# Turning the feed-forward's input with VectorE blocks and memory transfers instead of TensorE transposes

## The chip, the cores and the metric

One Trainium2 (trn2) chip; the kernel runs on 1 of its cores. The metric is the device time of one execution in microseconds, as the median of the runs. The engines are named as in the profile: PE (TensorE; PEld its weight loads), DVE (VectorE), ACT (ScalarE), POOL (GpSimd) and SP (SyncE, which issues all DMAs here; SPq is its queue).

## What is computed

x has 4096 tokens (2 sequences of 2048) of 256 features. An attention block with hierarchical decay (16 heads, 12 levels), a residual and a layer norm come first; a gated two-step cell over the two sequences, a residual and a layer norm follow. Everything is fp32.

```python
x = L0_attn_x                                    # (2, 2048, 256)
x = layernorm(x + attention(x, ...))             # 16 heads, chunks of 128 tokens in the kernel
# feed-forward: a scan over the first axis (2 steps), then one output product
ft = sigmoid(xt @ wf.T + c @ uf.T + bf)
it = sigmoid(xt @ wi.T + c @ ui.T + bi)
gt = tanh(xt @ wc.T + c @ uc.T + bc)
c  = ft * c + it * gt
h  = tanh(x @ wo.T + c_final @ uo.T + bo)
out = layernorm(x + h)
```

## The kernel before

**Tiles.** The normalised result of the attention stands in SBUF as `xs`, 32 chunks (`ci`) of 128 tokens, tokens on the partitions, 256 features along the row. The feed-forward needs x with features on the partitions, so it must be turned. It works in 4 blocks (`blk`) of 512 tokens for each of the two sequences (`t`); block (blk, t) holds the four chunks from 16t + 4 blk on. Every product is made of three (`mm3`): each operand is split into a rounded high part (`wH`, `yH`, by ACT) and the rest (`wL`, `yL`, by DVE or POOL).

**Turning before.** `turn_block(blk, t)` exists on three engines. PE makes 8 transposes (2 halves `k` of the features, 4 chunks) through `tr` (L386) into two PSUM banks; ACT copies each bank to `yH` (fp32r); DVE subtracts `yH` from the bank to give `yL`. Then `gate_x` multiplies them with the weights.

**Order.** Each engine's program is written out by hand over steps `s` from -3 to 140; a chunk of attention takes four steps. An engine works strictly in the order of its program and stands at a wait until the semaphore is there. Chunk ci is normalised by DVE in `outer_norm(ci)` at step 4ci + 11, so chunk 28 at step 123, chunk 29 at 127, and 31 at 135. The feed-forward begins at step 127 (`FIRST_FFN`) and is laid out as groups by `ffn_groups()`, one group a step: first the turns of (0,0) and (0,1), then gate products; the turns of the later blocks stand in later groups.

**ACT near the seam.** At steps 119 to 126 ACT splits the eight feed-forward weights, `split_ffn(0)` to `split_ffn(7)`, and at step 124 (ahead of `split_ffn(5)`) it makes the exponentials `E` of the last chunk (31), for which PE's scores of that chunk wait. So the splits of weights 2, 3 and 4 stand ahead of these exponentials in ACT's program. PE's `first_bias` (36 products of two columns) follows at step 126 and needs weights 3 to 5. POOL subtracts for `wL` behind ACT.

**SP's queue.** For each pair of chunks `sg` it stores and reloads the coefficients (`load_coefs`: one store to `scr`, then 8 broadcast loads of 64 KB for each chunk), then issues `load_xt(sg + 3)` and `load_x(sg + 2)`. Weights 0 and 1 are loaded at sg 13 and 14; after sg 15 come `load_wf(2)` to `load_wf(7)`, each after the `wL` two before it, since `xt` has two buffers; then the output stores.

Of the kernel before, what the change touches and what calls it, by code (L numbers as in the profile page):

```python
# [5 lines left out]
P = 128  # L6
F32 = mybir.dt.float32
F32R = mybir.dt.float32r
# [136 lines left out]
TURN = {u[1:]: n for n, u in enumerate([u for u in UNITS if u[0] == "t"])}  # L145
YUSE = {u: n for n, u in enumerate([u for u in UNITS if u[0] == "t" or (u[0] == "o" and u[1] < 16)])}

# [8 lines left out]
def program(nc, x, xT, wqk, wtok, wout, wffn, cst, bcv, fv, out):  # L156
    ctx = ExitStack()
    with ctx:
        scr = nc.dram_tensor("scr", (8, 8, 2, 128), F32, kind="Internal").ap()

        def sb(name, shape, dt=F32):
# [17 lines left out]
        oo = sb("oo", [P, 256])  # L179
        x1 = sb("x1", [P, 256])  # L180
        st1 = sb("st1", [P, 6])
        mv1 = sb("mv1", [P, 2])
# [50 lines left out]

        yH, yL = [[[sb(f"{n}{t}{i}", [P, 2, 512], F32R) for i in range(2)] for t in range(2)] for n in ("yH", "yL")]
        gb = [[sb(f"g{i}{n}", [P, 512]) for n in range(3)] for i in range(2)]
# [8 lines left out]
        ring = [banks[0:3], [banks[3], banks[6], banks[7]]]  # L244

        def turned(blk, k):

            return banks[4 + k] if blk or not k else banks[6]


# [14 lines left out]
        l_xt = [sem(f"l_xt{i}") for i in range(2)]  # L265
        l_sc, l_cB = sem("l_sc"), [sem("l_cB0"), sem("l_cB1")]
        l_x = [sem(f"l_x{i}") for i in range(NSG)]

# [3 lines left out]
        g_v0, g_s0 = sem("g_v0"), sem("g_s0")  # L272
        p_b0, p_turn, p_gate, p_o = sem("p_b0"), sem("p_turn"), sem("p_gate"), sem("p_o")

# [13 lines left out]
        d_b0, d_y, d_c1, d_c2 = sem("d_b0"), [sem("d_y0"), sem("d_y1")], sem("d_c1"), sem("d_c2")  # L288
        d_c2l, d_mv3, d_out = sem("d_c2l"), sem("d_mv3"), sem("d_out")

        g_xl, g_sp, g_vw = sem("g_xl"), sem("g_sp"), sem("g_vw")
# [13 lines left out]
        def _(e):  # L305
# [10 lines left out]
            def load_coefs(sg):  # L316
# [5 lines left out]
                for c in range(2):  # L322
                    ci = 2 * sg + c
                    if ci in INTER:
# [4 lines left out]
                        for a in range(8):  # L329
                            e.dma_start(cB[c][16 * a:16 * a + 16, :, :, :].rearrange("p l u t -> p (l u) t"),  # L330
                                        scr[a, :, c, :].partition_broadcast(16)).then_inc(l_cB[c], 16)

            load_xt(0)
            e.dma_start(wt0, kt(wtok)).then_inc(l_wt, 16)
# [17 lines left out]
            for sg in range(NSG):  # L352
                load_coefs(sg)
                if sg + 3 < NSG:
                    e.wait_ge(g_xl, sg + 1)
                    load_xt(sg + 3)
                if sg + 2 < NSG:
                    load_x(sg + 2)
                if sg >= NSG - 3 and sg < NSG - 1:
                    e.wait_ge(g_xl, sg + 1)  # L360
                    load_wf(sg - NSG + 3)
            for n in range(2, 8):
                e.wait_ge(g_wf, n - 1)
                load_wf(n)
            for n in range(16):
                e.wait_ge(a_out, n + 1)
                if n == 15:
                    e.wait_ge(d_out, 1)
                e.dma_start(ov[:, :, n, :], xs[:, n:n + 17:16, :]).then_inc(l_out, 16)
# [11 lines left out]
        def _(e):  # L381
# [221 lines left out]

            def turn_block(blk, t):
                e.wait_ge(d_x2, 16 * t + 4 * blk + 4)
                if blk == 0 and t == 0:

                    e.wait_ge(d_w, 4 * NC)
                for k in range(2):
                    use = YUSE["t", blk, t]  # L610
                    if use:
                        e.wait_ge(d_y[k], use)
                    elif k == 1:
                        e.wait_ge(m_free[0], len([m for m, u in MISC.values() if m == 0]))
                    if blk == 1 and t == 0 and k == 1:

                        e.wait_ge(d_oo, NC)
                    for q in range(4):
                        y = tr(turned(blk, k)[:, 128 * q:128 * q + 128], xs[:, 16 * t + 4 * blk + q, 128 * k:128 * k + 128])
                    y.then_inc(p_turn, 1)  # L620

            def gate_x(blk, t, mt, n):
                y, idx = blk % 2, 4 * blk + 2 * t + mt
                if idx >= 2:
                    e.wait_ge(a_g, 3 * (idx - 2) + n + 1)
                elif n == 0:
                    e.wait_ge(d_b0, 1)
                if n == 0:
                    e.wait_ge(d_y[1], YUSE["t", blk, t] + 1)
                if idx == 1 and n == 1:  # L630

                    e.wait_ge(d_y[1], 2)
                if idx == 1 and n == 2:
                    e.wait_ge(m_free[1], len([m for m, u in MISC.values() if m == 1]))
                for k in range(2):
                    c = wcol(WF + n, mt)
                    m = mm3(ring[mt][n][:, :], wH[:, k, c], wL[:, k, c], yH[t][y][:, k, :], yL[t][y][:, k, :],
                            k == 0, k == 1 and not t)
                if not t:
                    m.then_inc(p_gate, 1)  # L640
# [25 lines left out]
            def outputs(n):  # L666
                blk, q = n // 4, n % 4
                y, use = blk % 2, YUSE["o", n]
                c = slice(128 * q, 128 * q + 128)
                Ba, Bb = [banks[i] for i in LAST.get(n, (4, 5))]  # L670
                if n in (12, 14, 15):

                    e.wait_ge(a_g, 48 if n == 12 else 51)
                else:
                    e.wait_ge(d_y[1], use if n < 12 else use - 1)
                for t in range(2):
                    for k in range(2):
                        m = mm3(Bb[:, 256 * t:256 * t + 256], yH[t][y][:, k, c], yL[t][y][:, k, c],
                                wH[:, k, wcol(WO)], wL[:, k, wcol(WO)], k == 0, k == 1)
                m.then_inc(p_o, 1)  # L680
                if blk < 3:
                    e.wait_ge(g_c2l, 2 * blk + 2)
                else:
                    e.wait_ge(d_c2l, 2 if n < 14 else 3)
                for k in range(2):
                    m = mm3(Ba[:, 0:256], c2H[y][:, k, c], c2L[y][:, k, c], wH[:, k, wcol(UO)], wL[:, k, wcol(UO)],
                            k == 0, k == 1)
                m.then_inc(p_o, 1)
# [14 lines left out]
            for s in STEPS:  # L703
# [31 lines left out]
                for u in units_at(s):  # L735
                    if u[0] == "x":
                        gate_x(*u[1:])
                    elif u[0] == "c":
                        gate_c(*u[1:])
                    elif u[0] == "h":  # L740
                        gate_h(*u[1:])
                    elif u[0] == "t":
                        turn_block(*u[1:])
                    elif u[1] < 16:
                        outputs(u[1])
# [3 lines left out]
        def _(e):  # L749
# [104 lines left out]
            def turn_block(blk, t):  # L854
                i = blk % 2
                for k in range(2):
                    e.wait_ge(p_turn, 2 * TURN[blk, t] + k + 1)
                    if blk >= 2 and k == 0:
                        e.wait_ge(p_o, 2 * (4 * (blk - 2) + 4))
                    act(yH[t][i][:, k, :], turned(blk, k)[:, :], ACT.Copy).then_inc(a_yh, 1)  # L860

# [41 lines left out]
            def outputs(n):  # L903
                i = n % 2
                e.wait_ge(d_y[1], YUSE["o", n] + 1)
                act(hh[i][:, :], hh[i][:, :], ACT.Tanh).then_inc(a_hh, 1)
# [73 lines left out]
        def _(e):  # L980
# [159 lines left out]
            def outer_norm(ci):  # L1140
                e.wait_ge(g_rs2, ci + 1)
                e.tensor_scalar(xs[:, ci, :], x1[:, :], mv2[:, 0:1], rs2[:, 0:1], ALU.subtract, ALU.mult).then_inc(d_x2, 1)

            def tokens(sg, j):
                nonlocal made
# [73 lines left out]
            def turn_block(blk, t):  # L1219
                i = blk % 2  # L1220
                for k in range(2):
                    e.wait_ge(a_yh, 2 * TURN[blk, t] + k + 1)
                    tt(yL[t][i][:, k, :], turned(blk, k)[:, :], yH[t][i][:, k, :], ALU.subtract).then_inc(d_y[k], 1)

# [35 lines left out]
            def outputs(n):  # L1260
                i, use = n % 2, YUSE["o", n]
                Ba, Bb = [banks[i] for i in LAST.get(n, (4, 5))]
                e.wait_ge(p_o, 2 * n + 2)
                if n >= 2:
                    e.wait_ge(d_y[1], YUSE["o", n - 2] + 1)
                tt(cu[i][:, :], Ba[:, 0:256], bv[:, B_BO:B_BO + 256], ALU.add).then_inc(d_y[0], 1)
                h3 = hh[i][:, :].rearrange("p (t n) -> p t n", t=2)
                e.wait_ge(d_y[0], use + 1)
                if n >= 2 and n - 2 != 13:
# [40 lines left out]
            for s in STEPS:  # L1310
# [37 lines left out]
                if (ci := chunk_at(s, 11)) is not None:  # L1348
                    outer_norm(ci)


# [224 lines left out]
```

## Time and profile before

| | |
|---|---|
| median of the runs | 687.79 us (687.26 to 689.74, 3 runs) |
| profiled execution | 687.91 us, span 686.1 us |
| mean granted clock of PE | 0.985 |
| PE busy | 665.7 us (97%) |
| DVE / ACT / POOL busy | 474.0 / 339.3 / 348.1 us |
| DMA | 53588 packets, 37.09 MB |

All times of the rows below are from the start of the span. In a timeline row stand start, duration, engine, line of the kernel, operation, result and operands, how many instructions are merged, and in brackets how long the engine was idle before and on whom it waited last. A clock of 1.00 is the 2.4 GHz level of PE, 0.50 the 1.2 GHz level.

### The profile page before, as it was taken

How to read it: one execution, taken by the hardware profiler on the slowest of the kernel's cores; microseconds unless marked ns; L12 is line 12 of the kernel's file. 1: busy time of each engine (PE TensorE's matmuls, PEld its weight loads, DVE VectorE, ACT ScalarE, POOL GpSimd, SP SyncE). 2: the span in 40 equal slices, each digit the busy share in tenths (PEclk: the TensorE clock that was granted, in tenths of full speed). 3: DMA queues.
4: the chain of work that ended last, by engine and by line, in shares of the span. 5: the costliest groups of instructions: out<-in, count | busy, mean ns of one | idle time of the engine just before them, and what ended most of it. 6: DMA issues, size and time to landing. Idle time of an engine off the chain costs nothing.

```text
span 686.1 us, 22147 instructions
## 1 busy us (share of the span) xinstructions
PE 665.7 (97%) x9194; PEld 602.8 (88%) x9194; DVE 474.0 (69%) x1072; ACT 339.3 (49%) x759; POOL 348.1 (51%) x471
## 2 busy tenths in 40 slices
PE   9999999999999999999999999999978999999994
PEld 7889999999999999899999999999967788888894
DVE  3765786869786868658696868688896445454546
ACT  5565444454555454544545555545433434555555
POOL 2715563647556565556474555665455215343434
PEclk9999999999999999999999999999997899999998
DMA  9213030302222130203031221303032000000002
GB/s 299 61 29 91 8 97 8 94 24 76 50 51 55 46 83 18 67 6 95 22 79 47 54 52 48 88 13 84 2 99 62 1 1 1 32 32 32 32 32 92
DMA packets 53588, 37.09 MB, mean 54 GB/s; under 512 B 5360, under 2 KB 52080, under 8 KB 53488
## 3 DMA queue, kind: packets, MB, share of 16 engines
q1 hardware_dynamic: 53488, 35.67, 19.1%
q8 instruction: 73, 1.20, 0.8%
q14 instruction: 27, 0.22, 0.1%
HBM read 30.41 MB, written 5.24 MB: 52 GB/s over the span
## 4 chain that ended last, share of the span: by engine, by line
PE 90%; DVE 3%; ACT 2%; SPq 1%; DMA 1%; issue 1%; POOL 1%; DVEq 0%; ACTq 0%; POOLq 0%
PE bank L383 66%; PE bank L386 6%; PE bank L407 5%; PE bank L474 5%; PE bank L439 5%; PE bank L503 4%; SPq L330 1%; DMA xt<-in_wffn 1%; DVE t L985 1%; ACT t L751 1%; ACT E L751 0%; DVE t L988 0%; DVE st L1285 0%; DVE hh L985 0%; DMA scr<-cT 0%
## 5 line engine op out<-in xcount | busy, mean ns | idle before, releaser
L383 PE MATMUL bank<-xH,wH 128*128 128x256 f32 x480 | 144.4, 301 | 1.2 <-ACT KT L751 0.9
L383 PE MATMUL bank<-xL,wH 128*128 128x256 f32 x480 | 135.0, 281 | 0.0
L383 PE MATMUL bank<-xH,wL 128*128 128x256 f32 x480 | 134.4, 280 | 0.0
L985 DVE TENSOR_TENSOR W<-bank,E 128x512 f32<-128x512 f32 x128 | 82.2, 685 | 31.3 <-PE bank L383 31.3
L383 PEld LDWEIGHTS bank<-xH,wH 128*128 128x128 f32 x480 | 90.4, 188 | 7.6 <-issue 7.0
L383 PEld LDWEIGHTS bank<-xL,wH 128*128 128x128 f32 x480 | 90.6, 189 | 0.4
L383 PEld LDWEIGHTS bank<-xH,wL 128*128 128x128 f32 x480 | 90.5, 188 | 0.0
L751 ACT ACTIVATE E<-bank 128x512 f32<-128x512 f32 x128 | 66.1, 604 | 47.7 <-PE bank L407 47.7
L751 ACT ACTIVATE QT<-bank 128x512 f32<-128x512 f32 x64 | 38.2, 596 | 101.3 <-PE bank L383 101.3
L383 PE MATMUL bank<-QT,KT 64*128 64x128 f32 x1024 | 65.8, 278 | 1.6 <-ACT E L751 1.6
L383 PEld LDWEIGHTS bank<-QT,KT 64*128 64x128 f32 x1024 | 59.7, 188 | 6.0 <-ACT E L751 1.8
L751 ACT ACTIVATE KT<-bank 128x512 f32<-128x512 f32 x64 | 38.0, 594 | 51.4 <-PE bank L383 51.4
L1357 POOL TENSOR_TENSOR lr<-mv,cs 128x1 f32<-128x1 f32 (+1 forms) x80 | 18.2, 227 | 80.9 <-DVE mv L1138 75.0
L1357 POOL TENSOR_TENSOR rs<-lr,cs 128x1 f32<-128x1 f32 (+1 forms) x80 | 51.7, 647 | 6.3
L1357 POOL TENSOR_TENSOR x<-oo,xs 128x256 f32<-128x256 f32 x32 | 23.5, 735 | 60.3 <-DVE oo L988 57.7
L1357 POOL TENSOR_TENSOR t<-t 128x416 f32<-128x416 f32 x42 | 46.6, 1110 | 3.4
L985 DVE TENSOR_TENSOR g<-g 128x512 f32<-128x512 f32 (+1 forms) x26 | 17.6, 676 | 38.3 <-ACT g L751 38.0
L407 PE MATMUL bank<-CT,AT 32*128 32x128 f32 x1024 | 38.1, 286 | 5.7 <-DVE CT L1212 4.1
L751 ACT ACTIVATE t<-t 128x416 f32<-128x416 f32 x64 | 35.3, 552 | 14.2 <-DVE t L1170 10.4
L1357 POOL TENSOR_TENSOR prod<-ll,cs 128x512 f32<-128x512 f32 x32 | 40.7, 1272 | 1.2 <-DVE ll L985 1.2
L1357 POOL TENSOR_TENSOR xL<-xt,xH 128x512 fp32r<-128x512 f32 x15 | 19.1, 1273 | 41.4 <-ACT xH L751 41.4
L383 PE MATMUL bank<-yH,wH 128*128 128x512 f32 (+1 forms) x102 | 40.1, 393 | 0.0
(151 smaller groups left out, 1678.0 us busy)
## 6 DMA issues: line engine op xcount, KB each, us to landing
cB<-scr SPq DMA_DIRECT2D x240, 64.0 KB, 2.9
xt<-in_xT SPq DMA_DIRECT2D x16, 256.0 KB, 2.9
xs<-in_x SPq DMA_DIRECT2D x16, 256.0 KB, 3.2
out<-xs SPq DMA_DIRECT2D x16, 256.0 KB, 2.1
xt<-in_wffn SPq DMA_DIRECT2D x8, 256.0 KB, 3.1
QT<-in_wqk SPq DMA_DIRECT2D x4, 256.0 KB, 5.8
KT<-in_wqk SPq DMA_DIRECT2D x4, 256.0 KB, 7.1
scr<-cT SPq DMA_DIRECT2D x16, 64.0 KB, 1.9
```

Source lines behind the costliest of these rows:

```text
L330: e.dma_start(cB[c][16 * a:16 * a + 16, :, :, :].rearrange("p l u t -> p (l u) t"), scr[a, :, c, :].partition_broadcast(16)).then_inc(l_cB ...
L383: return e.matmul(o, a, b, start=start, stop=stop)
L386: return e.transpose(o, i, ident)
L407: m = e.matmul(XP[q][:, :].rearrange("p (h t) -> p h t", h=H)[:, :, 8 * j:8 * j + 8], AT[b][r, j, :], CT[b][r, :].rearrange("p (h t) -> p ...
L439: y = e.matmul(YB[32 * n:32 * n + 32, 128 * k:128 * k + 128], V[sg % 3][:, c, v:v + 32], W[:, h, :], start=u == 0 and k == 0, stop=u == 1, ...
L474: t = e.matmul(MB[MISC["inter", ci, k][0]][32 * n:32 * n + 32, 128 * i:128 * i + 128], S[r, l, n, 16 * o:16 * o + 32], QT[b][r, 4 * o + n, ...
L503: t = e.matmul(MB[m][k:k + 64, 16 * q:16 * q + 16], Kt[:, 128 * q + k:128 * q + k + 64], Vw[b][:, c, 128 * h + 16 * q:128 * h + 16 * q + 1 ...
L751: return e.activation(o, i, f, **kw)
L985: return e.tensor_tensor(o, a, b, op)
L1357: return e.tensor_tensor(o, a, b, op)
```

## The change

The eight transposes of a block leave PE. After `outer_norm(ci)` DVE turns the chunk in blocks of 32x32 (`turn_result`, one `transpose` of 128x256 into one of two buffers `tx`); SP stores that to a scratch tensor `xscr` in memory (128 rows of 1 KB), and `load_turned(blk, t)` brings a block back with features on the partitions: 8 DMAs, each 32 partitions x 16 x 32 numbers, that is 512 runs of 128 bytes. ACT and DVE split `yT` from SBUF in place of the PSUM banks. PE's `turn_block` and its wait on the normalisation go; the wait for the last `W` moves to the first gate product. Semaphores and memory are added accordingly; `yT` has one buffer for each t, so a load waits for the split of the block before (`d_yl`).

In SP's queue `store_turned(2 sg - 3)` and `store_turned(2 sg - 2)` stand behind `load_coefs(sg)`, `load_turned(0, 0)` behind `load_wf(2)` and `load_turned(0, 1)` behind `load_wf(3)`; blocks 1 and 2 come after `load_wf(7)`, block 3 after the first two output stores.

```diff
+            def store_turned(ci):
+                e.wait_ge(d_tx, ci + 1)
+                e.dma_start(xscr[4 * ci:4 * ci + 4, :, :].rearrange("i f c -> (i f) c"), tx[ci % 2][:, :]).then_inc(
+                    l_tx[ci % 2], 16)
+
+            def load_turned(blk, t):
+
+                c0 = 16 * t + 4 * blk
+                for i in range(2):
+                    e.wait_ge(l_tx[i], 16 * (c0 // 2 + 2))
+                if blk == 0:
+
+                    e.wait_ge(p_proj, 8 * NSG)
+                else:
+                    e.wait_ge(d_yl, TURN[blk - 1, t] + 1)
+                s4 = xscr[4 * c0:4 * c0 + 16, :, :].rearrange("g f (k j t) -> j f k g t", k=2, j=4)
+                for j in range(4):
+                    for k in range(2):
+                        e.dma_start(yT[t][32 * j:32 * j + 32, k, :].rearrange("f (g t) -> f g t", g=16),
+                                    s4[j, :, k, :, :]).then_inc(l_yT[t], 16)
...
             for sg in range(NSG):
                 load_coefs(sg)
+                for ci in (2 * sg - 3, 2 * sg - 2):
+                    if ci >= 0:
+                        store_turned(ci)
                 if sg + 3 < NSG:
...
             for n in range(2, 8):
                 e.wait_ge(g_wf, n - 1)
                 load_wf(n)
+                if n in (2, 3):
+                    load_turned(0, n - 2)
+            for blk in (1, 2):
+                for t in range(2):
+                    load_turned(blk, t)
+                for ci in (NC - 3, NC - 2) if blk == 1 else (NC - 1,):
+                    store_turned(ci)
             for n in range(16):
+                if n == 2:
+                    for t in range(2):
+                        load_turned(3, t)
...
             def gate_x(blk, t, mt, n):
                 y, idx = blk % 2, 4 * blk + 2 * t + mt
                 if idx >= 2:
                     e.wait_ge(a_g, 3 * (idx - 2) + n + 1)
                 elif n == 0:
                     e.wait_ge(d_b0, 1)
+
+                    e.wait_ge(d_w, 4 * NC)
                 if n == 0:
-                    e.wait_ge(d_y[1], YUSE["t", blk, t] + 1)
...
+                    e.wait_ge(d_yl, TURN[blk, t] + 1)
...
+            def turn_result(ci):
+
+                e.wait_ge(d_x2, ci + 1)
+                if ci >= 2:
+                    e.wait_ge(l_tx[ci % 2], 16 * (ci // 2))
+                e.transpose(tx[ci % 2][:, :], xs[:, ci, :]).then_inc(d_tx, 1)
```

## Rows read from the trace of the kernel before

**Rows 1.** The page's part 4: shares of the span in the chain, by line

```profile
PE bank L383 66%; PE bank L386 6%; PE bank L407 5%; PE bank L474 5%; PE bank L439 5%; PE bank L503 4%; SPq L330 1%; DMA xt<-in_wffn 1%; DVE t L985 1%; ACT t L751 1%; ACT E L751 0%; DVE t L988 0%; DVE st L1285 0%; DVE hh L985 0%; DMA scr<-cT 0%
```

**Rows 2.** The chain in order of time, 560 on: start, us, what

```profile
560.07 0.87 PE bank L386 x8
...
630.79 0.87 PE bank L386 x8
```

**Rows 3.** Timeline 526 to 536, where attention ends and the feed-forward begins

```profile
528.68 1.97 PE L386 MATMUL bank<-cs,xs 128*128 128x128 f32 x8
528.86 0.16 DVE L985 TENSOR_TENSOR b<-bank,fvs 128x6 f32<-128x6 f32 x1 [0.81 <-PE bank L383]
...
530.46 0.69 DVE L985 TENSOR_TENSOR yL<-bank,yH 128x512 fp32r<-128x512 f32 x1 [1.44 <-ACT yH L751]
...
533.17 1.94 PE L439 MATMUL bank<-W,V 128*32 128x128 f32 x32
...
535.04 0.80 PE L383 MATMUL bank<-yH,wH 128*128 128x512 f32 x1
```

**Rows 4.** Stretches: length, busy us by engine, PE's clock, DMA share, GB/s

```profile
466.00:476.00 10.00, 10.00 (x152) 9.24 (x153) 8.24 (x18) 6.54 (x15) 7.07 (x9) 1.00 0.47 96
584.00:588.00 4.00, 4.00 (x28) 3.64 (x27) 1.76 (x4) 1.52 (x4) 1.55 (x4) 1.00 0.20 66
514.00:516.00 2.00, 2.00 (x34) 1.52 (x34) 1.93 (x4) 0.00 (x0) 1.92 (x3) 0.51 0.40 118
528.00:530.00 2.00, 2.00 (x10) 2.00 (x11) 0.21 (x2) 0.17 (x1) 1.87 (x3) 0.50 0.00 0
```

**Rows 5.** Timeline of SP's queue, 439 to 524: start and length of the issues

```profile
439.65 3.70 SPq L330 DMA_DIRECT2D cB<-scr  x8
...
508.50 14.28 SPq L313 DMA_DIRECT2D xt<-in_wffn  x6
```

**Rows 6.** Timeline of ACT, 511 to 526

```profile
511.78 1.30 ACT L751 ACTIVATE wH<-xt 128x512 fp32r<-128x512 f32 x2 [7.46 <-DMA xt<-in_wffn]
516.86 0.63 ACT L751 ACTIVATE wH<-xt 128x512 fp32r<-128x512 f32 x1 [3.78 <-DMA xt<-in_wffn]
517.39 2.04 ACT L751 ACTIVATE E<-bank 128x512 f32<-128x512 f32 x4
...
525.20 0.63 ACT L751 ACTIVATE wH<-xt 128x512 fp32r<-128x512 f32 x1 [2.94 <-DMA xt<-in_wffn]
```

**Rows 7.** Timeline of DVE, 475 to 516, and of POOL at 512

```profile
475.58 0.59 DVE L988 SCALAR_TENSOR_TENSOR t<-pre,t 128x416 f32<-128x416 f32 x1 [1.05 <-POOL t L1357]
...
491.69 1.29 DVE L985 TENSOR_TENSOR W<-bank,E 128x512 f32<-128x512 f32 x2 [1.73 <-PE bank L383]
...
500.38 0.74 DVE L985 TENSOR_TENSOR S<-S,dec 128x256 f32<-128x256 f32 x2
...
513.01 2.44 DVE L985 TENSOR_TENSOR S<-S,dec 128x256 f32<-128x256 f32 x2
...
515.82 0.41 DVE L1142 TENSOR_SCALAR xs<-x,mv,rs 128x256 f32<-128x256 f32 x1
...
512.49 2.69 POOL L1357 TENSOR_TENSOR wL<-xt,wH 128x512 fp32r<-128x512 f32 x2 [2.14 <-ACT wH L751]
```

**Rows 8.** Timeline of PE, 500 to 519

```profile
500.63 1.08 PE L439 MATMUL bank<-W,V 128*32 128x128 f32 x32
...
512.16 1.78 PE L407 MATMUL bank<-CT,AT 32*128 32x128 f32 x32 [3.82 <-DVE CT L1212]
513.87 1.94 PE L439 MATMUL bank<-W,V 128*32 128x128 f32 x32
...
518.51 2.13 PE L383 MATMUL bank<-QT,KT 64*128 64x128 f32 x32 [1.59 <-ACT E L751]
```

**Rows 9.** Groups by line, engine and form: count, busy us, mean ns, idle before

```profile
L985 DVE TENSOR_TENSOR W<-bank,E 128x512 f32<-128x512 f32 x128 | 82.2, 685 | 31.3 <-PE bank L383 31.3
...
L1212 DVE STREAM_TRANSPOSE CT<-C 128x512 f32<-128x512 f32 x32 | 22.8, 711 | 1.1
```

## What I expect, and why

> **What bounds the kernel now.** I read the chain of work that ended last first, on the page: PE's lines hold 91% of the span, 66% its product line L383 and 6% L386, the line through which every TensorE transpose goes [rows 1]. Work taken from PE is therefore worth its full time wherever PE is the chain. Second, the same chain in order of time over the feed-forward: PE without a break up to 668, with a piece "L386 x8" of 0.87 us six times, the first at 560.07 and the last at 630.79 [rows 2]. Each is one block of 512 tokens being turned. Third, the timeline at the seam between attention and feed-forward, where the first two blocks are turned: PE turns at 528.68, but the first gate product starts only at 535.04 [rows 3]. Fourth, the queues that the change adds work to: SP's DMA issues [rows 5], what ScalarE waits for behind them [rows 6], VectorE and GpSimd [rows 7] and PE [rows 8] from 500 to 525. That last reading decides the case.
>
> **What is removed: six turns inside the feed-forward.** PE is the chain there, so 6 x 0.87 = 5.2 us go [rows 2], if the turned data is there in time. It should be: a pair of loads is issued as soon as the block before has been split, some 28 us before its own use (560.07 against about 532, where the first split ends [rows 2, 3]), and a pair needs about 14 us (below). ScalarE's copy and VectorE's subtraction stay, now from SBUF, where a subtraction can be slowed by GpSimd as below; neither engine is the chain there. Cost 0; if that cover is gone, the price is the same 5.2 us back.
>
> **What is removed at the seam.** Before, from the end of the bias products (528.68) to the first gate product (535.04) pass 6.4 us: two turns, their copies and subtractions, then the last chunk's weighing (1.94) [rows 3]. After the change PE goes from the bias to the weighing at once. Beside that, VectorE adds the bias (0.16) and makes two subtractions (0.69 each), 1.5 us and a few hand-overs; ScalarE's copies can run before, since it idled from 525.8 on [rows 3, 6]. So 1.9 to 2.0 us remain of 6.4: a gain of 4.4 us. Two things take from it. The 32 weighing products took 1.08 us at 500.63 and 1.94 at 513.87, where the granted clock was 0.51 (the 1.2 GHz level) after PE had stood still for 3.8 us before 512.16 [rows 4, 8]. The wait that I find below makes PE stand still longer, so the scores and the inter-chunk products that follow it start at that level: some 3.8 us (512.16 to about 516) at half speed, 1.8 us lost. And the gate products start sooner after the bias stretch, in which the clock was at 0.50 too [rows 4], so more of them run slowly: 0 to 1.7 us, I take 0.8. Net gain 1.8 us.
>
> **What is added on VectorE.** 32 transposes of 128x256. One of 128x512 takes 711 ns; a pass over 256 columns takes 0.41 against 0.69 for 512, so 711 - 280 = 430 ns, with the wait for its own normalisation about 0.46 [rows 7, 9]: 15 us in all. It stands right behind the normalisation. What follows there is a wait in both kinds of chunk: 1.73 us for PE's scores in one, 1.05 us for GpSimd in the other [rows 7]. Both are longer than 0.46, so I take 0; the upper bound is what 0.1 us a chunk would make, 3 us. The stores, 32 of 128 KB, are few and long pieces: 0.
>
> The Trainium skill ("VectorE: DVE Perf Modes", The three transpose paths) gives TensorE 390 ns for a 128x128 bf16 transpose and VectorE 311 ns for 32x32 blocks only. Here PE's eight fp32 transposes cost 0.87 us together in the chain, 109 ns each, so the trace disagrees with the first figure as a price. By the rows the 64 turns are worth 7.0 us of PE, by the page's figure 25, and the forecast would be 680 instead of 698; the measurement decides.
>
> **What is added on SP's queue, and who stands behind it.** SP issues in order and waits in order. Up to now load_wf(2) goes out at 508.50, right after the last coefficient loads [rows 5], and ScalarE, waiting, splits that weight at 511.78, 3.3 us later [rows 6]. In the change three things stand ahead of what follows:
>
> - store_turned(28), before load_wf(2): it waits for VectorE to have normalised chunk 28 and turned it. That normalisation is at 515.82 to 516.23. The pair of S products ahead of it took 2.44 us in place of the 0.74 of a chunk before, beside GpSimd's subtractions of wL (512.49 to 515.18) [rows 7]; those are now later, so 1.7 us fall away: normalised at 514.5, turned at 515.0, stored at 515.4, load_wf(2) at 515.5. That is 7.0 us later than 508.50 (8.7 if the 1.7 stay).
> - load_turned(0,0), between load_wf(2) and load_wf(3), and load_turned(0,1), between load_wf(3) and load_wf(4): 8 DMAs each, 512 pieces of 128 bytes in each DMA, so 4096 pieces, 256 to each of 16 DMA engines.
>
> Nothing in the trace moves 128-byte pieces, so I bound them. Issue: eight coefficient DMAs go out in 3.70 us [rows 5], so a load takes 3.7 us at least. Pieces: from 466 to 476, 16 coefficient DMAs of 128 pieces of 512 bytes kept the engines 0.47 busy: 0.47 x 16 x 10 / 2048 = 37 ns a piece. From 584 to 588, one output of 256 pieces of 1 KB: 0.20 x 16 x 4 / 256 = 50 ns [rows 4]. A line through the two gives 24 ns without any bytes and 27 ns at 128 bytes: 256 x 27 = 7.0 us for one load, more than its issue. The ends are 3.7 us (by issue) and 9.5 us (37 ns, as dear as 512 bytes). I take 7.0, since the line goes through both rows.
>
> The weights go through the same queues behind these pieces: load_wf(2) lands at 518.8, then 7.0 + 0.8 (16 pieces of 50 ns) to load_wf(3), and again 7.8 to load_wf(4): 534.4. ScalarE's program has the splits of weights 2, 3 and 4 ahead of the exponentials of the last chunk: its trace shows 516.86 and right behind it 517.39, after 3.78 us of waiting for that DMA [rows 6]. So the exponentials start at 534.9 in place of 517.39, 17.5 us later. PE's scores of chunk 31 wait for them (518.51, 1.59 us idle already now [rows 8]), and all that is left of attention waits for the scores. PE has nothing else to do: the feed-forward's products stand behind in its order and need the weights anyway.
>
> **Sum.** 686.1 + 17.5 - 1.8 - 5.2 = 696.6 us of span; the profiled execution took 687.91 with 1.8 outside its span, and the median of the runs is 687.79, within 0.1 of it. Forecast: 698.4 us. With loads bound by issue (3.7 us each, wf(4) issued at 523.7) the exponentials start 10.1 us later: 691.0. With 9.5 us a load: 703.4; with the 1.7 us of relief gone and 3 us on VectorE, 708.
>
> **The rivals.**
>
> - Faster. The pieces and the stores are hidden: ScalarE reaches the exponentials of chunk 31 no later than now, because the weights land in time. Then only the gains count, 4.4 less 0.7 for the clock at the gates, and 5.2: 687.9 - 8.9 = 679.0. It decides at load_wf(4) landing by about 517, and for that load_wf(2) would have to go out 7 us before the store ahead of it can. For it speaks that PE, not DMA, has the chain; against it, ScalarE's waits of 7.46 and 3.78 us for these very loads [rows 6]: there is no slack to hide them in.
> - No change. The delay is at its least (small pieces free, every issue a little shorter than above: the exponentials 9 us late) and the seam gives its full 4.4 us: 687.9 + 9 - 4.4 - 5.2 = 687.3.
> - Much slower. A piece of 128 bytes costs more than one of 512, say twice the 27 ns: 54 x 256 = 13.8 us a load, 13.6 more for the two: 712.0. The later loads, 28 us a pair against 28 us of time, would then be just in time. No row shows pieces under 512 bytes in number.
>
> The Trainium skill says of this last case ("DMA: Bandwidth & Descriptors", Specifications) that transfers under 512 bytes are not at line rate, being read-modify-write. No run here shows it yet.
>
> **How the numbers follow.** Forecast (690 to 708): 0.68. Much slower: 0.19. No change: 0.06. Faster: 0.07. A measurement of this kernel tells about 0.5% (3.4 us) from no change. Faster is then 0.07, same 0.06, slower 0.87. The range reaches from just under the issue-bound sum, 689, into the dear pieces, 712.
>
> **What would show it.** In the profile after: load_wf(2) issued near 515.5; ScalarE idle for long before wH, put down to the DMA of in_wffn; the first E of chunk 31 near 535; PE idle before its scores some 17 us, at half the clock behind it; VectorE's transposes near 430 ns; no "L386 x8" in the feed-forward, and 5 us less from the first gate product to the end (151.1 us before [rows 3]). The forecast is wrong if the exponentials start before 527, if a load of 4096 pieces takes under 4 or over 10 us, or if PE waits inside the feed-forward.

## The result, and the profile after

| | before | after |
|---|---|---|
| median, runs taken together | 687.52 us | 694.58 us (694.11 to 695.32) |
| ratio | | 1.0101, 95% interval 1.0085 to 1.0117 |
| span of the profiled execution | 686.1 us | 693.6 us |
| mean granted clock of PE | 0.985 | 0.973 |

The changed kernel is 1.0% slower. 698.4 had been forecast, with 689 to 712 as its range. TensorE does less (659.8 us busy in place of 665.7), and the kernel takes longer.

The seam between attention and feed-forward is where to look. First SP's queue in the changed kernel, from 508 on (start, length and number of the issues); it answers [rows 5]:

```profile
508.26 7.88 SPq L337 DMA_DIRECT2D xscr<-tx  x2
516.19 0.43 SPq L315 DMA_DIRECT2D xt<-in_wffn  x1
516.73 4.23 SPq L353 DMA_DIRECT2D yT<-xscr  x8
521.01 0.49 SPq L315 DMA_DIRECT2D xt<-in_wffn  x1
521.61 4.30 SPq L353 DMA_DIRECT2D yT<-xscr  x8
525.95 9.53 SPq L315 DMA_DIRECT2D xt<-in_wffn  x4
```

The two stores (L337) hold the queue for 7.9 us, nearly all of it the wait for chunk 28: the first store goes out at 508.26, the second, that of chunk 28, at 515.81. Weight 2 goes out at 516.19, not 508.50. Then each reload of a turned block (L353, eight DMAs) puts 4.3 us ahead of the next weight. ScalarE stands behind that, in its timeline (in brackets how long it was idle, and on whom it waited), against [rows 6]:

```profile
519.65 0.63 ACT L769 ACTIVATE wH<-xt 128x512 fp32r<-128x512 f32 x1 [15.00 <-DMA xt<-in_wffn]
524.64 0.63 ACT L769 ACTIVATE wH<-xt 128x512 fp32r<-128x512 f32 x1 [4.36 <-DMA xt<-in_wffn]
529.58 0.63 ACT L769 ACTIVATE wH<-xt 128x512 fp32r<-128x512 f32 x1 [4.31 <-DMA xt<-in_wffn]
530.12 2.04 ACT L769 ACTIVATE E<-bank 128x512 f32<-128x512 f32 x4
```

And PE's timeline behind ScalarE, against [rows 8]:

```profile
516.83 1.10 PE L422 MATMUL bank<-cs,KT 128*128 128x128 f32 x8
531.24 3.78 PE L419 MATMUL bank<-QT,KT 64*128 64x128 f32 x32 [13.31 <-ACT E L769]
534.95 3.19 PE L510 MATMUL bank<-QT,S 64*32 64x128 f32 x128
```

The last exponentials start 12.7 us later than before (517.39), PE stands still for 13.3 us, and the scores behind that take 3.78 us in place of 2.13. The clock is in the stretches of the changed kernel (length, busy us by engine, granted clock, DMA share, GB/s):

```profile
517.00:522.00 5.00, 0.92 (x8) 0.68 (x7) 0.00 (x0) 0.63 (x1) 1.26 (x1) 0.83 0.83 155
522.00:527.00 5.00, 0.00 (x0) 0.00 (x0) 0.00 (x0) 0.63 (x1) 1.57 (x3) 0.50 0.84 153
531.00:537.00 6.00, 5.76 (x112) 5.54 (x120) 1.29 (x2) 3.37 (x8) 2.71 (x4) 0.50 0.25 75
537.40:544.00 6.60, 6.60 (x120) 6.13 (x104) 5.57 (x13) 3.07 (x6) 2.55 (x4) 1.00 0.02 5
546.00:551.00 5.00, 5.00 (x12) 3.94 (x13) 1.77 (x4) 0.69 (x1) 0.21 (x1) 0.50 0.49 78
551.00:556.00 5.00, 5.00 (x22) 4.03 (x22) 2.49 (x5) 2.42 (x4) 0.33 (x1) 1.00 0.81 128
```

Scores and inter-chunk products run at 0.50 (the 1.2 GHz level), the bias products after 537.4 at 1.00 (2.4 GHz), and the gate products start at 0.50 again, until 551. Last, the start of the feed-forward in the timeline of all engines, against [rows 3]:

```profile
542.15 2.50 POOL L1388 TENSOR_TENSOR wL<-xt,wH 128x512 fp32r<-128x512 f32 x2
543.04 1.08 PE L475 MATMUL bank<-W,V 128*32 128x128 f32 x32
543.48 3.52 DVE L1007 TENSOR_TENSOR yL<-yT,yH 128x512 fp32r<-128x512 f32 x4
545.94 0.77 PE L419 MATMUL bank<-yH,wH 128*128 128x512 f32 x1 [1.82 <-DVE yL L1007]
```

From there on the chain is PE without a turn in it, where [rows 2] had one of 0.87 us six times; the chain in order of time shows it as one piece:

```profile
545.94 129.61 PE bank L419 x688
```

To compare all kernels I cut each profiled execution at three points: A, the start of the exponentials of chunk 30; B, that of chunk 31; C, the first gate product. The column on the clock is how long it still stood at half just behind C. A moves by up to 1.5 us from run to run, from well before the seam, so the parts behind it say more than the span. Each row is one execution, up to 1.5 us from the median of its kernel (e1 was taken 1.1 below, e6 1.5 above), so the medians decide what a kernel is worth, and the rows only where its time lies.

| kernel | to A | A to B | B to C | C to end | at half clock after C | span |
|---|---|---|---|---|---|---|
| before | 500.77 | 16.6 | 17.6 | 151.1 | 1.4 | 686.1 |
| after | 501.10 | 29.0 | 15.8 | 147.7 | 5.1 | 693.6 |
| e1_both_moved | 501.33 | 18.7 | 14.4 | 146.9 | 3.4 | 681.3 |
| e2_store_late | 501.14 | 23.0 | 15.6 | 147.6 | 4.9 | 687.4 |
| e3_loads_spread | 500.87 | 25.0 | 14.6 | 147.0 | 3.7 | 687.5 |
| e4_turns_added | 501.71 | 15.5 | 16.4 | 151.3 | 1.8 | 684.9 |
| e5_wait_added | 501.84 | 22.7 | 18.1 | 150.5 | 0 | 693.1 |
| e6_loads_later | 502.25 | 16.8 | 13.1 | 147.2 | 4.1 | 679.3 |
| e7_sixth_first | 502.23 | 15.7 | 13.3 | 146.0 | 1.5 | 677.3 |
| e8_filled | 501.40 | 29.5 | 13.1 | 147.3 | 4.1 | 691.2 |
| e9_long_pieces | 502.11 | 27.0 | 15.8 | 147.6 | 5.0 | 692.5 |
| e10_weights_sooner | 501.69 | 15.8 | 16.2 | 146.0 | 1.5 | 679.7 |

After against before: 0.3 + 12.4 - 1.8 - 3.4 = 7.5 us, the whole difference of the spans.

### The profile page after: what moved, and what is told of

The parts are those of the page before. It is cut to its first block, busy times and chain, and to the rows that moved or that the text cites. A ratio compares the mean times of both kernels' runs of the same rounds, so it can differ in the third digit from the quotient of the medians.

```text
span 693.6 us, 22178 instructions
## 1 busy us (share of the span) xinstructions
PE 659.8 (95%) x9130; PEld 597.7 (86%) x9130; DVE 488.3 (70%) x1104; ACT 339.3 (49%) x759; POOL 349.1 (50%) x471
## 4 chain that ended last, share of the span: by engine, by line
PE 88%; DVE 6%; ACT 2%; SPq 1%; issue 1%; DMA 1%; POOL 0%; DVEq 0%; ACTq 0%; POOLq 0%
PE bank L419 65%; PE bank L510 5%; PE bank L443 5%; PE bank L422 5%; PE bank L475 4%; PE bank L539 4%; SPq L353 1%; DVE zt L1007 1%; DVE t L1007 1%; ACT t L769 1%; DMA xt<-in_wffn 1%; DVE W L1007 0%; ACT E L769 0%; DVE t L1010 0%; DVE yL L1007 0%
## 5 line engine op out<-in xcount | busy, mean ns | idle before, releaser
L419 PE MATMUL bank<-QT,KT 64*128 64x128 f32 x1024 | 67.5, 283 | 13.3 <-ACT E L769 13.3
L419 PEld LDWEIGHTS bank<-QT,KT 64*128 64x128 f32 x1024 | 61.3, 192 | 17.7 <-ACT E L769 13.6
L1007 DVE TENSOR_TENSOR g<-g 128x512 f32<-128x512 f32 (+1 forms) x26 | 17.6, 679 | 34.1 <-ACT g L769 33.8
L419 PE MATMUL bank<-yL,wH 128*128 128x512 f32 (+1 forms) x102 | 39.9, 391 | 0.0
```

The lines of the kernel that those rows point to most:

```text
L419: return e.matmul(o, a, b, start=start, stop=stop)
L1007: return e.tensor_tensor(o, a, b, op)
```

## The experiments

My theory is that SP's order is the loss: what stands ahead of load_wf(4) in its queue holds back the last exponentials. The rivals: VectorE's transposes, the small pieces, the clock.

### Both moved out of the way (e1_both_moved)

The store of chunk 28 goes behind the last weight; the loads of block 0 go where SP waited anyway.

```diff
                 for ci in (2 * sg - 3, 2 * sg - 2):
-                    if ci >= 0:
+                    if 0 <= ci < NC - 4:
                         store_turned(ci)
...
                 load_wf(n)
-                if n in (2, 3):
-                    load_turned(0, n - 2)
+                if n in (3, 5):
+                    load_turned(0, n // 5)
+            store_turned(NC - 4)
```

> The changed kernel with SP's order alone edited: the store of chunk 28 goes out after the last weight load, the two loads of block 0 stand behind load_wf(3) and load_wf(5), where SP waited for GpSimd before the change. Theory 1 (SP's order is the whole loss): load_wf(2) goes out at 508 to 509, the exponentials of chunk 31 start at 517.5 to 518.5 (530.1 in the changed kernel, 517.4 in the one before), and the gains are then all that is left: 680 to 682.5 us, 5 to 7.5 below the kernel before. Theory 2 (the transposes, the small pieces or the clock are the loss, wherever the loads stand): the exponentials move, but the time stays at 688 or more. Theory 3 (GpSimd's subtractions of weights 6 and 7 collide with VectorE's first subtractions of yT): the first gate product starts later than 14.5 us after the exponentials.

Measured: 684.14 us, ratio 0.9957 to the kernel before (0.9942 to 0.9971). Slower has become faster by the order of one queue alone. But it is 1.6 us over my upper bound, and the exponentials started at 520.04, 1.5 us later than forecast. SP's queue of this kernel says why:

```profile
509.24 0.98 SPq L315 DMA_DIRECT2D xt<-in_wffn  x2
510.33 5.95 SPq L353 DMA_DIRECT2D yT<-xscr  x8
516.33 1.01 SPq L315 DMA_DIRECT2D xt<-in_wffn  x2
```

Where I put the load, SP had waited some 4 us for GpSimd (from 509.7 to 513.8 in the kernel before); the load took 5.95 us, and weight 4 went out at 516.33, not 513.8. Not all of these 2.5 us are the queue's: GpSimd itself was ready only at 515.05, since weight 2 landed 1.3 us later than in the kernel before (513.05, not 511.76). Theory 2 falls. By the mark that I had set for theory 3 it is not borne out: the first gate product came 14.4 us after the exponentials, not later than 14.5. The collision that it names is in the traces all the same; e7 looks at it.

### Each move alone (e2_store_late, e3_loads_spread)

e2 has the first and the last of these edits without the middle one, e3 the middle one alone.

> The changed kernel with the store of chunk 28 alone moved behind the last weight load; the loads of block 0 stay between weights 2, 3 and 4. Theory 1: the wait of 7.4 us for the transpose of chunk 28 goes (load_wf(2) near 508.7), two loads of 4.3 us of issue stay: load_wf(4) out near 518.3, the exponentials near 522.5, 7.6 earlier than in the changed kernel: 686 to 688 us. If the small pieces and not the issue set the loads, load_wf(3) lands more than 3.5 us after its issue.

Measured: 688.24 us, ratio 1.0017 (1.0005 to 1.0029), 0.2 over the range I gave. Weight 4 went out at 520.22 and the exponentials started at 524.15, both later than the 518.3 and 522.5 I had written: load_wf(2) was 0.8 later, and one issue of the second load took 1.51 us in place of 0.49.

> The changed kernel with the loads of block 0 alone moved, behind load_wf(3) and load_wf(5); the store of chunk 28 stays ahead of load_wf(2). Theory 1: load_wf(2) still near 516.2, then only one load of 4.3 us ahead of load_wf(4): the exponentials near 525.5 to 526, 4.4 earlier than in the changed kernel: 689 to 691.5 us. The two moves together should give about the sum of the two alone.

Measured: 689.53 us, ratio 1.0039 (1.0024 to 1.0053), with the exponentials at 525.88: both as forecast.

From A to B the store's move takes 6.0 us off, the loads' move 4.0, both together 10.3; the changed kernel has 12.4 more than the kernel before. So the wait for chunk 28 is worth 6 us and the loads ahead of weights 3 and 4 another 6, of which e1 still keeps 2. The two moves alone add up to 10.0 us, together they gave 10.3.

### The wait alone, in the old kernel (e5_wait_added)

```diff
                 e.wait_ge(g_wf, n - 1)
+                if n == 2:
+                    e.wait_ge(d_x2, NC - 3)
                 load_wf(n)
```

> The kernel before, with one wait added: load_wf(2) waits on SP until VectorE has normalised chunk 28, as the store of that chunk makes it wait in the changed kernel; nothing else is changed. Theory 1: load_wf(2) goes out near 514.6 instead of 508.5, the exponentials start near 523.5, the kernel gets slower by 6 us, and by 1 to 2 more for products at half the clock after the longer stand of PE: 693.5 to 696 us. Theory 2 (the wait is covered by other work): within 1 us of 687.5.

Measured: 695.41 us, ratio 1.0120 (1.0105 to 1.0135). The time is in the range of theory 1. One semaphore wait, which adds no work at all, costs 8.3 us in the median. Of the 7.0 in the profiled span 6.1 lie from A to B and 0.4 at the seam; 1.1 lie ahead of A, where nothing was edited, and 0.6 come back behind C with the clock. Weight 2 went out at 515.96 and the exponentials started at 524.55, 1.4 and 1.0 us later than forecast. SP's queue and ScalarE in this kernel:

```profile
515.96 13.97 SPq L313 DMA_DIRECT2D xt<-in_wffn  x6
...
524.01 0.63 ACT L753 ACTIVATE wH<-xt 128x512 fp32r<-128x512 f32 x1 [3.45 <-DMA xt<-in_wffn]
524.55 2.04 ACT L753 ACTIVATE E<-bank 128x512 f32<-128x512 f32 x4
```

### The transposes alone (e4_turns_added)

```diff
+            def turn_result(ci):
+                e.wait_ge(d_x2, ci + 1)
+                if ci >= 2:
+                    e.wait_ge(d_tx, ci - 1)
+                e.transpose(tx[ci % 2][:, :], xs[:, ci, :]).then_inc(d_tx, 1)
...
                     outer_norm(ci)
+                    turn_result(ci)
```

> The kernel before with VectorE's 32 transposes of 128x256 added behind the normalisations, into two spare buffers that nobody reads; no store, no load, TensorE's turns stay. Theory 1 (they fall into waits of 1.05 and 1.73 us): 0 to 0.4 us more, 687.1 to 687.6; the exponentials of chunk 31 at most 0.4 us later. Theory 2 (VectorE, 70% busy, has no room for 14 us more): up to 3 us slower, 690.

Measured: 688.12 us against 687.54, ratio 1.0010 (0.9998 to 1.0023): 0.5 us over the range of theory 1, not told from no change, and 1.6 us at the most. Most of the 14.2 us of work went into waits. The group of the transposes in this kernel and two of VectorE's waits show it (of a wait stand us in all, times and the longest). The one is for TensorE's scores ahead of W, 31.3 us in [rows 9]; the other is for GpSimd, once 1.05 us in [rows 7]:

```profile
L1150 DVE STREAM_TRANSPOSE tx<-xs 128x256 f32<-128x256 f32 x32 | 14.2, 445 | 1.1
...
DVE W L987 <- PE bank L385: 25.1, 16, 3.1
DVE t L990 <- POOL t L1366: 15.5, 11, 2.9
```

The first fell by 6.2 us. The second had been 20.8 us in the kernel before and fell by 5.3:

```profile
DVE t L988 <- POOL t L1357: 20.8, 11, 3.4
```

### No load ahead of weight 4 (e6_loads_later), and GpSimd out of VectorE's way (e7_sixth_first)

e6 is e1 with the loads at n in (5, 7). e7 adds to that, in GpSimd's program at step 125 (`NG` is 128), the subtraction for weight 6, which step 125 had behind the root (`split_wf` holds the lines that stood there):

```diff
+                if s == NG - 3:
+                    split_wf(6)
                 if (ci := chunk_at(s, 9)) is not None:
                     e.wait_ge(d_mv2, ci + 1)
                     root(rs2[:, :], lr2[:, :], mv2[:, 1:2], g_rs2)
```

> As e1_both_moved, with the two loads of block 0 behind load_wf(5) and load_wf(7), so that none stands ahead of load_wf(4). Theory 1: load_wf(4) goes out at 514 to 514.5 again (516.33 in e1), the exponentials start at 517.5 to 518 (520.04 in e1), and the first gate product about 14.4 us behind them: 681.5 to 683 us. Rival (the second load now lands too late): the first gate product comes later than 15.5 us after the exponentials, or PE waits for yL in the first groups, and the time is that of e1, 684.

Measured: 679.56 us, ratio 0.9886 (0.9871 to 0.9901), 2 us better than I expected, though weight 4 went out at 515.00 and the exponentials started at 519.00, 0.5 and 1.0 us past what I had written. A to B is nearly that of the kernel before (16.8 against 16.6), and the seam is shorter (13.1): the last scores took 2.1 us at the full clock, where they took 3.5 in e1 at half of it.

> As e6_loads_later, with GpSimd's subtraction for weight 6 put ahead of the root for chunk 29, for which it waits on VectorE; so it is done before VectorE's first subtraction of yT. In the changed kernel that subtraction took 1.72 us beside GpSimd's two, in place of 0.68. Theory 1 (the two engines get in each other's way with two operands in SBUF): the first yL takes 0.7 to 1.2 us, the first gate product comes 0.5 to 1 us earlier than in e6, and the time falls by as much. Rival (the first yL is long for another reason, such as the wait for the bias): it stays at 1.6 to 1.7 us and nothing moves.

Measured: 679.13 us, ratio 0.9884 (0.9871 to 0.9898). VectorE's timeline in e6 and, behind it, in e7:

```profile
529.61 3.53 DVE L1008 TENSOR_TENSOR yL<-yT,yH 128x512 fp32r<-128x512 f32 x4
```

```profile
529.78 1.29 DVE L1008 TENSOR_TENSOR yL<-yT,yH 128x512 fp32r<-128x512 f32 x2
531.47 1.29 DVE L1008 TENSOR_TENSOR yL<-yT,yH 128x512 fp32r<-128x512 f32 x2 [0.41 <-ACT yH L770]
```

Four in 3.53 us, the first of them 1.72, against two in 1.29: the collision is real. But it was moved and not removed. The forecast 0.5 to 1 us did not come: the two intervals lie on each other, and B to C is 13.3 us where e6 had 13.1. GpSimd's subtraction for weight 6 now stands beside VectorE's `zs`, which takes 1.37 us in place of 0.42. So `oo` comes 0.95 us later behind the `zt` products than in e6, and TensorE's weighing waits for it. The rows of e7, of VectorE, GpSimd and PE:

```profile
525.67 1.37 DVE L1008 TENSOR_TENSOR zs<-zt 128x256 f32<-128x256 f32 x1
525.22 1.54 POOL L1389 TENSOR_TENSOR wL<-xt,wH 128x512 fp32r<-128x512 f32 x1 [2.35 <-ACT wH L770]
529.29 1.94 PE L476 MATMUL bank<-W,V 128*32 128x128 f32 x32 [0.82 <-DVE oo L1008]
```

The Trainium skill ("SBUF — State Buffer", SBUF: two separate sides) states that VectorE, with two inputs in SBUF, and a GpSimd instruction that reads SBUF share a pair of ports, which the one that starts first holds for its whole instruction while the other stands. The rows of e6 agree: the first subtraction of yT starts at 529.61, 0.1 us after one of GpSimd's, and ends at 531.34, 0.55 us after that one's end, where one alone takes 0.68.

### PE kept busy (e8_filled)

```diff
+                    if n == 1 and ci == NC - 1:
+                        e.wait_ge(a_qk, 8 * NSG)
+                        for _ in range(100):
+                            mm(banks[0][:, 256:512], wtH[:, 0, 0:128], wtH[:, 0, 0:256])
                     if n == 1:
                         scores(ci, 0)
```

> The changed kernel with 100 extra products of 128x128 by 256 columns ahead of the scores of chunk 31, into an unused half of a bank that nobody reads: PE works where it stood still for 13.3 us. Theory 1 (the stand lowers the clock, and what follows pays for it): the clock stays at its upper level until the bias, the scores take 2.1 us in place of 3.78 and the inter-chunk products 2.0 in place of 3.19, and the time falls by 1.5 to 3 us to 691.5 to 693. Rival (the clock costs nothing here, since the wait for VectorE's W and zt covers it): the two get shorter but the time stays within 0.7 us of 694.6.

Measured: 692.36 us, ratio 1.0075 (1.0061 to 1.0089), so 2.2 us less than the changed kernel for 100 useless products, and in the range of theory 1. PE in this kernel, where the clock is at 1.00 from 518 to 537:

```profile
518.09 12.22 PE L419 MATMUL bank<-wtH 128*128 128x256 f32 x100
532.01 2.14 PE L419 MATMUL bank<-QT,KT 64*128 64x128 f32 x32 [1.70 <-ACT E L773]
534.15 2.02 PE L510 MATMUL bank<-QT,S 64*32 64x128 f32 x128
```

Scores and inter-chunk products took 2.8 us less together, and B to C is 2.7 shorter. The rival falls: VectorE's part behind them, from the first `zt` to the gates, takes 7.8 us in both kernels and only moved forward with them.

### Long pieces (e9_long_pieces)

```diff
-                s4 = xscr[4 * c0:4 * c0 + 16, :, :].rearrange("g f (k j t) -> j f k g t", k=2, j=4)
+                s4 = xscr[4 * c0:4 * c0 + 16, :, :].rearrange("(i g) f c -> i (g f c)", i=8).rearrange(
+                    "i (p n) -> i p n", n=512)
                 for j in range(4):
                     for k in range(2):
-                        e.dma_start(yT[t][32 * j:32 * j + 32, k, :].rearrange("f (g t) -> f g t", g=16),
-                                    s4[j, :, k, :, :]).then_inc(l_yT[t], 16)
+                        e.dma_start(yT[t][32 * j:32 * j + 32, k, :], s4[2 * j + k, :, :]).then_inc(l_yT[t], 16)
```

> The changed kernel with each of the 64 reload DMAs moving the same 64 KB in 32 runs of 2 KB in place of 512 runs of 128 bytes; the data comes in the wrong order, so the feed-forward's input is not the one of the reference, and everything else is as it was. Theory 1 (a reload is bound by the issue of its eight DMAs, not by its pieces): the issues take 0.44 us or more each as against 0.49, load_wf(3) goes out 4 us or more after load_wf(2) (4.8 in the changed kernel), the exponentials of chunk 31 move by less than 1 us, and the time stays at 693.5 to 695. Theory 2 (pieces of 128 bytes are what costs, as the prediction had it): a reload gets at least 2 us cheaper and the time falls by 4 us or more to 690.5.

The reload of this kernel leaves out the right order of the data. Measured: 693.7 us, ratio 1.0093 (1.0075 to 1.0111), against 694.58 and 1.0101: in the range of theory 1, and its interval covers most of the changed kernel's. SP's queue:

```profile
517.20 0.43 SPq L315 DMA_DIRECT2D xt<-in_wffn  x1
517.74 3.68 SPq L354 DMA_DIRECT2D yT<-xscr  x8
521.46 0.43 SPq L315 DMA_DIRECT2D xt<-in_wffn  x1
522.00 3.65 SPq L354 DMA_DIRECT2D yT<-xscr  x8
```

With a sixteenth of the pieces the eight issues still take 3.7 us. From A to B 2.0 us go in the profiled execution, twice what theory 1 allowed: 1.3 in the issues, the rest in weight 4, which lands 2.9 us after its issue and not 3.6. So the pieces cost 2 us at this place, and 0.9 in the medians, which is not told from nothing. The sixteen issues still take 7.3 us. That they would take less if there were fewer of them is not shown: no run has fewer, larger DMAs.

### Weights sooner (e10_weights_sooner)

```diff
                 for c in range(2):
                     ci = 2 * sg + c
+                    if ci == NC - 1:
+                        for n in (2, 3):
+                            e.wait_ge(g_wf, n - 1)
+                            load_wf(n)
...
-            for n in range(2, 8):
+            for n in range(4, 8):
...
-                if s == NG - 3:
-                    split_wf(6)
+                if s in (NG - 7, NG - 3):
+                    split_wf(s - NG + 9)
```

> As e7_sixth_first, with load_wf(2) and load_wf(3) put between the coefficient loads of chunks 30 and 31, where their buffers are already free, and GpSimd's subtraction for weight 2 ahead of the root for chunk 28. Theory 1 (SP's order sets when the last exponentials start, in both directions): load_wf(2) goes out at 503 to 504, load_wf(4) at 510 to 512, the exponentials start at 515 to 516 in place of 517.9, limited now by PE's exponents: 676.5 to 678 us. Rival (the exponentials are held by something else, such as the coefficient loads, now later): nothing moves, 679.1.

Measured: 681.07 us, ratio 0.9911 (0.9894 to 0.9927): slower than e7 by 1.9 us, where 676.5 to 678 had been forecast. The weights did come sooner (load_wf(2) at 504.47, weight 4 at 512.19), and a new wait took their place. VectorE and PE in this kernel:

```profile
512.88 1.04 DVE L1239 COPY C<-ll 128x64 f32<-128x64 f32 x1
513.85 0.67 DVE L1241 TENSOR_REDUCE C<-prod 128x128 f32<-128x512 f32 x1
514.55 0.71 DVE L1246 STREAM_TRANSPOSE CT<-C 128x512 f32<-128x512 f32 x1
...
515.32 2.09 PE L448 MATMUL bank<-CT,AT 32*128 32x128 f32 x32 [6.05 <-DVE CT L1246]
517.34 1.94 PE L480 MATMUL bank<-W,V 128*32 128x128 f32 x32
```

GpSimd's subtractions for weights 2 and 3 now ran from 509.5 to 513.9, beside VectorE's way to CT, and stretched it: a copy of 128x64 took 1.04 us, where it took 0.18 in the changed kernel, and `zs` 1.37 in place of 0.42. PE waited 6.05 us for CT, where it had waited 3.82 [rows 8] and 4.25 in e7, and what it did then ran at half the clock, until 521.5. The exponentials started at 517.48, held now by PE, and the scores behind them at 521.10 and not 519.48 as in e7, since PE came to them late; so the loss lies from B to C (16.2 against 13.3). Both theories miss this: SP's order no longer set the time here.

## Why the prediction was right, and where not

- **The store of chunk 28 ahead of the weights**: right. Chunk 28 turned at 515.0 and load_wf(2) at 515.5 were forecast; 515.8 and 516.19 came. The relief of 1.7 us came too, as the S products took 0.74 us without GpSimd beside them; but VectorE reached them 0.8 us later than in the kernel before (513.79, not 513.01).
- **A load of 4096 pieces**: the mis-sized term. 7.0 us by a line through pieces of 512 bytes and 1 KB; it took 4.3 us, near the lower end (3.7, by issue). The line was drawn through shares of busy time, 37 ns a piece from 466 to 476. There a piece of 512 bytes took an engine 38 ns in the mean; over the whole trace of the kernel before, the median is 27, and for 1 KB it is 46. A line through these gives 13 ns at 128 bytes, not 27, and 13 is the median of the changed kernel's pieces. From 517 to 527 the engines were busy for (0.83 + 0.84) x 5 x 16 = 134 us with 8192 pieces and some weights: 16 ns a piece at the most. By the landings, weights 2, 3 and 4 came at 519.63, 524.62 and 529.56, about 5.0 us apart where 7.8 had been forecast: 5.6 of the 17.5 us too much; with weight 2 landed 0.8 later than forecast, 12.7 is left. Both bounds were from rows; between them I should have leaned on the issue, which was measured on like DMAs, and not on a line drawn outside its two points.
- **The seam**: 4.4 us less 1.8 were forecast from B to C, 15.0 us; 15.8 came. The sum is nearly right, and that is in part luck, since three of its terms were off. The loss at half clock was foreseen, but is 2.7 (e8) and not 1.8. From the end of the bias products to the first gate product 2.9 us are left and not the forecast 1.9 to 2.0: missing was GpSimd beside the first subtraction of yT, 1.0 us; I had written that down for the feed-forward and left it out here. And 1.1 us that I had not forecast came back: the clock stood at its upper level throughout the bias products, from 537.35 on, where it had fallen at 526.2 before, within them. They and the product ahead of them take 4.97 us, from 538.07 to 543.04, where it was 6.08, from 522.60 to 528.68. The first rows of that stretch, before and after:

```profile
522.60 1.13 PE L383 MATMUL bank<-wo,yt 128*128 128x256 f32 x4
...
538.07 1.13 PE L419 MATMUL bank<-wo,yt 128*128 128x256 f32 x4
```

- **The clock at the gates**: 0.8 taken, 0 to 1.7 bounded; it cost more than the bound. 5.1 us ran at half clock in place of 1.4, and half of the difference is 1.8. The other rows of the table bear out this price: e6 has 2.6 us more of slow clock than e7 and 1.2 us more from C to the end.
- **The turns in the feed-forward**: right. At the same 1.5 us of slow clock after C, e7 and e10 have 146.0 where the kernel before has 151.1: 5.1 us, for 6 x 0.87 = 5.2. The changed kernel shows only 3.4 of it, because of those 1.8.
- **The transposes on VectorE**: right. 445 ns for 430, no cost that can be told (e4), the bound of 3 us too wide.
- **Small pieces dear**: wrong. A block of 512 KB took 4.3 us to issue, 122 GB/s, and the pieces kept pace with the issue: 256 of 13 ns are 3.3 us. The Trainium skill ("DMA: Bandwidth & Descriptors", Specifications) says that transfers under 512 bytes miss the line rate. The trace agrees so far: 128 bytes in 13 ns are 10 bytes a ns of an engine, 1 KB in 46 ns are 22. It does not bear out a price high enough for this rival, which needed 54 ns a piece.
- **Faster, or no change**: wrong for this kernel, yet e6 and e7 show that both gains of the faster rival exist: 8 us, once nothing stands ahead of weight 4.

In sum, to B, from B to C and from C to the end: forecast 17.5 - 2.6 - 4.4 = 10.5 us of span, measured 12.7 - 1.8 - 3.4 = 7.5. The mechanism and its place were those forecast. That the median is only 3.8 us off 698.4, and the span 3.0 off, is partly luck: 4.8 too much in the wait for the weights was made up in part by 0.8 too little at the seam and 1.0 too little for the clock at the gates.

## What to carry to other kernels

SP's queue works in order, so a store that waits for an engine is a wait for all loads behind it (8.3 us for one wait in e5); ask of each DMA put into a queue what is queued behind it, and which engine, working in order too, stands at that. Removing work from the bounding engine paid here only after the new transfers had been put behind the loads that the last chunk needs, weights 2 to 4: the same change gave +1.0% and, in another order, -1.1%. The eight DMAs of a load cost the queue 3.7 us even with long pieces and 4.3 with pieces of 128 bytes; look at the time to issue before the time of the pieces. And work taken off one engine's path can land beside another instruction on the same path, as GpSimd's subtraction did in e7 and e10.

## What the runs showed of the hardware

A piece of 128 bytes took a DMA engine 13 ns in the median (16 at the most by the busy share), one of 512 bytes 27, one of 1 KB 46. One issue took 0.46 us with 32 pieces of 2 KB (3.68 for eight) and 0.53 with 512 pieces of 128 bytes (4.23). Where a load of eight was issued right behind two weights (e1), its issues stretched to 5.95 us; why is not shown. VectorE's 32x32-block transpose took 445 ns for 256 columns and 711 for 512. Beside a GpSimd subtraction of 1.3 us, a VectorE subtraction of 128x512 took 1.72 us in place of 0.68, a copy of 128x64 1.04 in place of 0.18. Point A moved by 1.4 us between runs of kernels that are the same up to there (500.87 in e3, 502.25 in e6). Their starts differ: from 4.0 to 7.0 us PE began or ran 14 products in e3 and 9 in e6, and the record of the clock at its upper level begins at 4.85 us in e3 and at 7.15 in e6. No run was made to show that this is the whole cause.
